# Mixture-of-experts placing on one core: one-hot tables stored with a group's ten picks innermost

## What is computed

```
x = x + segment_sum(norm(x)[src] * edge_weight, dst) @ W.T + b                 # 100000 edges
x = x + ffn on the half of the nodes that a router picks
x = x + relu(segment_sum((norm(x) @ W_rel[type])[src] * gate * w, dst))        # 16 relations
# the last stage: mixture of 8 experts, two per node
gate_logits = norm(x) @ Wg + bg
top_w, top_i = top_k(gate_logits, 2); top_w = softmax(top_w)
out = sum over e of w_dense[:, e] * (gelu(norm(x) @ W1[e] + b1[e]) @ W2[e] + b2[e])
```

## Time and profile before

| What | Value |
|---|---|
| Median of 3 runs | 4001.26 us |
| Lowest and highest of the runs | 3999.29 and 4010.76 us |
| Profiled execution: span from the first to the last recorded instruction | 3402.6 us |
| Profiled execution: its own time around the span | not recorded; the median is 598.7 us above the span |
| Mean granted TensorE clock | 0.902 |
| Busy share: PE, weight loads, DVE, ACT, POOL | 77%, 56%, 51%, 21%, 55% |
| First gather, about | 79 to 1118 us |
| Second gather's loops, about | 1661 to 2670 us |
| Placing | 2678 to 2731 us |
| Experts | 2732 to 3402 us |

### The profile page before, as it was taken

One profiled execution on the slowest core, in us unless ns is written; L12 is line 12 of the kernel. 1 busy time (PEld: TensorE's weight loads), 2 busy tenths in 40 slices (PEclk: granted clock), 3 DMA queues, 4 the chain that ended last, 5 costly groups with the idle time before them and its releaser, 6 DMA issues. The chain is left out here.

```text
span 3402.6 us, 59974 instructions
## 1 busy us (share of the span) xinstructions
PE 2615.4 (77%) x14271; PEld 1921.6 (56%) x14272; DVE 1733.1 (51%) x5663; ACT 723.6 (21%) x1907; POOL 1869.7 (55%) x1915
## 2 busy tenths in 40 slices
PE   7688888887777799999655555564555389999997
PEld 6577777776665344444344444443444267767774
DVE  6455545454554655555355454544544544545553
ACT  4121111111110233333211010000000233333332
POOL 1777777777774000000377777777777245555554
PEclk9899999998999899999888888777777689999998
DMA  7333333333332444444545454555544623222232
GB/s 224 110 113 113 113 111 111 113 113 113 110 113 67 173 197 192 188 191 194 194 141 155 151 154 142 152 154 151 146 146 146 241 59 48 45 45 48 45 48 33
DMA packets 175589, 434.08 MB, mean 128 GB/s; under 512 B 41712, under 2 KB 103792, under 8 KB 169232
## 3 DMA queue, kind: packets, MB, share of 16 engines
q0 software_dynamic: 97072, 236.21, 26.9%
q1 hardware_dynamic: 57424, 183.78, 14.1%
q10 hardware_dynamic: 21008, 13.24, 1.3%
HBM read 275.05 MB, written 158.04 MB: 127 GB/s over the span
## 5 line engine op out<-in xcount | busy, mean ns | idle before, releaser
L776 POOL DMA_INDIRECT g_msg<-table,idx x1564 | 1517.3, 970 | 518.8 <-issue 476.5
L848 PE MATMUL psum<-g_msg,g_hot 128*128 x3328 | 967.4, 456 | 593.0 <-SPq L719 358.1
L848 PEld LDWEIGHTS psum<-g_msg,g_hot 128*128 128x128 f32 x3328 | 756.5, 233 | 789.5 <-issue 654.5
L796 DVE TENSOR_SCALAR g_hot<-iota,g_cols 128x128 f32<-128x128 f32 x1664 | 450.1, 364 | 31.9 <-DVE g_cols L793 30.5
L1908 POOL DMA_INDIRECT out<-ex_y,ex_to x112 | 206.0, 1839 | 253.9 <-DMA out<-ex_y,ex_to 165.3
L768 POOL MEMSET g_origin<- 128x256 f32 x1 | 0.3, 313 | 590.8 <-POOLq L1359 590.8
L1594 PE MATMUL psum<-wrel_halves,t_xhi 128*128 128x512 f16 x784 | 298.2, 380 | 1.7 <-DVE t_row L1475 1.7
L1595 PE MATMUL psum<-wrel_halves,t_xhi 128*128 128x512 f16 x784 | 298.1, 380 | 0.0
L1596 PE MATMUL psum<-wrel_halves,t_xlo 128*128 128x512 f16 x784 | 298.1, 380 | 0.0
L1475 DVE TENSOR_SCALAR t_row<-psum,t_gate 128x256 f32<-128x256 f32 x392 | 171.2, 479 | 233.7 <-PE psum L1596 231.7
L2074 PE MATMUL psum<-w,ex_ghi 128*128 x784 | 260.6, 382 | 6.7 <-DVE ex_y L1983 6.4
(11 more groups left out here) (353 smaller groups left out, 3231.7 us busy)
## 6 DMA issues: line engine op xcount, KB each, us to landing
table<-t_row SPq DMA_DIRECT2D x48, 2048.0 KB, 6.3
g_msg<-table,idx POOLq DMA_INDIRECT x1564
piece_stage<-in_w SPq DMA_DIRECT2D x32, 512.0 KB, 5.7
w_halves<-piece_halves SPq DMA_DIRECT2D x32, 512.0 KB, 3.4
w<-w_halves SPq DMA_DIRECT2D x8, 2048.0 KB, 22.6
rows<-sc_row ACTq DMA_DIRECT2D x50, 128.0 KB, 2.2
out<-acc ACTq DMA_DIRECT2D x49, 128.0 KB
table<-t_row SPq DMA_DIRECT2D x24, 256.0 KB, 2.5
```

The lines of the kernel that those rows point to most:

```text
L776: pool.indirect_dma_start(out=msg[:, at:at + D], out_offset=None, in_=table, in_offset=bass.IndirectOffsetOnAxis(ap=t[f"idx{g}"][:, n:n + ...
L796: last = nc.vector.tensor_scalar(hot[b][:, k * P:(k + 1) * P], t["iota32"][:, :], c3[:, k, where:where + 1], c3[:, k, weight:weight + 1], ...
L848: pe.matmul(ps, hot[b % PAIR][:, k * P:(k + 1) * P], msg[:, bass.ds(slot_at[k], D)], start=False, stop=False, skip_group_check=True).then_ ...
```

## The change

The innermost axis of `hot_tile`, `hot_row` and `parts` becomes the pick within the group (`LANES` is 10), for all groups; `by_lane` gives that view. ACT writes once a table `lanes` of 128 x 10 float16, in which each number stands ten times, and DVE compares it with the picks, which are now read with step one along the innermost axis and with step zero along the middle one. ACT's five instructions per group read and write pairs of float16 with a step of 20 bytes between the pairs. Both operands of PE's matmuls have a step of 20 bytes between elements. Besides, single register loads become `value_load`, and three wait values per batch on PE are masked with 1023.

```diff
@@ slot_number
-        _, (n,) = nc.values_load_multi_w_load_instructions(slot_at(m, 0, 1), engines=[eng.engine], min_val=0, max_val=WINDOWS,
-                                                           skip_runtime_bounds_check_because=sure)
-        return n
+        return eng.value_load(slot_at(m, 0, 1), min_val=0, max_val=WINDOWS)
@@ gather, tensor
-                    pe.wait_ge(tiles_in, code[MSG_TILES])
+                    pe.wait_ge(tiles_in, code[MSG_TILES] & 1023)
...
-                            pe.wait_ge(bank_free, code[BATCH + k // BANKS] + 1)
+                            pe.wait_ge(bank_free, (code[BATCH + k // BANKS] & 1023) + 1)
@@ gather, close_from
-                    _, (n,) = nc.values_load_multi_w_load_instructions(
-                        t["closed"][0:1, bass.ds(m, 1)], engines=[act.engine], min_val=0, max_val=WINDOWS - 1 - k,
-                        skip_runtime_bounds_check_because=sure)
+                    n = act.value_load(t["closed"][0:1, bass.ds(m, 1)], min_val=0, max_val=WINDOWS - 1 - k)
@@ class Place
+    LANES = GROUP * TOP
...
+        self.lanes = late.sb("pl_lanes", [P, P * self.LANES], F16)
...
+    def by_lane(self, x, n):
+
+        return x[:, :].rearrange("p (q s) -> p q s", s=self.LANES)[:, :, 0:n]
@@ Place.vector
+        dve.wait_ge(self.lanes_made, 1)
...
-                nc.vector.tensor_tensor(hot_[:, 0:n * width].rearrange("p (s q) -> p s q", q=width), t["iota16"][:, 0:width].unsqueeze(1).to_broadcast([P, n, width]),
-                                        pick[:, first:first + n].unsqueeze(2).to_broadcast([P, n, width]), ALU.is_equal).then_inc(done, 1)
+                nc.vector.tensor_tensor(self.by_lane(hot_, n), self.by_lane(self.lanes, n)[:, 0:width, :],
+                                        pick[:, first:first + n].unsqueeze(1).to_broadcast([P, width, n]), ALU.is_equal).then_inc(done, 1)
@@ Place.scalar
+        nc.scalar.activation(self.by_lane(self.lanes, self.LANES), t["iota16"][:, :].unsqueeze(2).to_broadcast([P, P, self.LANES]), ACT.Copy).then_inc(self.lanes_made, 1)
         act.wait_ge(self.exp_ready, 1)
...
-                cut = slice(k * TOP * PLACE_COLS, (k + 1) * TOP * PLACE_COLS)
-                last = nc.scalar.activation(self.parts[b][:, cut], self.hot_tile[b][:, cut], ACT.Copy, scale=self.const["number"][:, n % self.CYCLE:n % self.CYCLE + 1])
+                to, of = (self.by_lane(x[b], self.LANES)[:, :, k * TOP:(k + 1) * TOP] for x in (self.parts, self.hot_tile))
+                last = nc.scalar.activation(to, of, ACT.Copy, scale=self.const["number"][:, n % self.CYCLE:n % self.CYCLE + 1])
@@ Place.tensor
-                last = pe.matmul(self.psN[:, to * PLACE_COLS:(to + 1) * PLACE_COLS], self.hot_row[b][:, s * P:(s + 1) * P],
-                                 self.parts[b][:, s * PLACE_COLS:(s + 1) * PLACE_COLS],
+                last = pe.matmul(self.psN[:, to * PLACE_COLS:(to + 1) * PLACE_COLS], self.by_lane(self.hot_row[b], self.LANES)[:, :, s],
+                                 self.by_lane(self.parts[b], self.LANES)[:, :, s],
```

More of the change, by code:

```diff
@@ L1681, in __init__ @@
         (self.link, self.consts_in, self.hot_ready, self.exp_ready, self.exped, self.summed, self.facts_ready, self.facts_stored,
-         self.tile_done, self.row_done, self.parts_done, self.mm_done) = core.sems(*(f"pl_{k}" for k in (
-            "link", "consts_in", "hot_ready", "exp_ready", "exped", "summed", "facts_ready", "facts_stored", "tile_done", "row_done", "parts_done", "mm_done")))
+         self.tile_done, self.row_done, self.parts_done, self.mm_done, self.lanes_made) = core.sems(*(f"pl_{k}" for k in (
+            "link", "consts_in", "hot_ready", "exp_ready", "exped", "summed", "facts_ready", "facts_stored", "tile_done", "row_done", "parts_done", "mm_done", "lanes_made")))
         self.psD, self.psT, self.psN = core.bank[6], core.bank[7], core.bank[0]
+    def by_lane(self, x, n):
+        return x[:, :].rearrange("p (q s) -> p q s", s=self.LANES)[:, :, 0:n]
     def sync(self, sp):
```

## The result

| | before | after |
|---|---|---|
| median, us (4 runs each) | 4006.01 (3999.29 to 4012.14) | 4038.88 (4033.08 to 4049.62) |
| profiled execution: span, us | 3402.6 | 4041.8 |
| granted TensorE clock, mean | 0.902 | 0.816 |

A forecast was written before the change was run, and what follows sets the result against it. The prediction took POOL to pace the gathers and the facts' store behind the weight stream to end the placing. Terms -0.06 (earlier store) and +0.5 (register loads) gave +0.4 us on 4001.26: 4001.7 us, range 3997 to 4016.

The forecast's parts named there:

- the register loads: Checked loads add 0.17 us each, hidden beside POOL in the loops, bare only behind the last fetch: +0.5 us, bounds 0 to 1.5.
- The three masks per batch on PE are one register operation each, beside POOL too: 0: PE's masked wait values in the gathers: hidden beside POOL, 0 us, and 0.1 at the last batch.
- what DVE, PE and ACT do beside them costs nothing: Gathers run at POOL's pace, so the other engines' work beside the fetches is free until the last fetch is out.
- the three signs by which I wanted to see myself wrong: PE or DVE last at the barrier, L1801 over 0.62 us, or the release more than 2 us earlier.
- POOL's waits as before: Sign of being right: POOL in the gathers still waits for nothing but its own issuing between 1563 of 1564 fetches.
- register loads come bare in the loops: Rival: 108 loads at 0.17 us on PE cost 18 us, 4020 us, if POOL waits for ring buffers; chance 0.02.
- The rival on ACT's stepped pairs: Placing, L1801: 1.27 us per copy gives +33 us, 4034 us; chance 0.10 for over 12 us, 0.08 for 3 to 12.
- the compares: DVE's two compares per group in the placing run at twice the rate: 0.82 and 0.74 us, from 1482 and 1317 ns.
- the ramp: One ACT instruction of 1280 elements, 1.3 us, written some 17 us before DVE asks for it: costs nothing.
- DVE's 12.4 us: DVE's own work in the placing falls by 10 x 1.24 us, hidden by the weight stream and the store behind it.
- PE may take up to the pace, 2.6 to 2.7 us, at no cost: Placing: PE's ten loads and matmuls, 1.09 us per group, stay under 2 us with stepped operands, hidden behind ACT and the store.
- the 1.24 forecast: The facts' store is issued 1.24 us earlier, behind the first group's faster compares; term -0.06 us at the end.

The follow-up runs named there:

- 4000 group: Kernels timed together in which every kernel took 3950 to 4110 us, the kernel before 3997 to 4051 us.
- after_again: The change itself, timed again in a group with the kernel before at 3996.85 us: 4045.07 us, ratio 1.0118.
- after_lean: The change with slot number and closed window loaded unchecked and bounded by masks, against the kernel before at 3996.85 us: 4033.80 us, ratio 1.0099.
- 3400 group: Kernels timed together in which every kernel, the kernel before included, took about 3400 us.
- after_third: The change itself once more, in a group with the kernel before at 3402.45 us: 3403.55 us, ratio 1.0001.
- regs_only: The kernel before with the change's three register edits and none of its placing, kernel before at 3399.90 us: 3400.51 us, ratio 1.0007.
- regs_again: The kernel before with only the change's register edits, timed again, kernel before at 3996.85 us: 4047.93 us, ratio 1.0132.

## Why the prediction was wrong

**Where the time goes.** In one 4000 group the change is 48 us above before and its register work alone 51, the same within the spread. With 0.058 us per operation, PE's three masks per batch are 3 x 208 x 0.058 = 36 us, an estimate as rough as that price; the 11 us between `after_again` and `after_lean` go with the assertions and their subtractions on PE, DVE and ACT, which no run here splits by engine. Together 47.

**The step that failed** is in the register loads: "The three masks per batch on PE are one register operation each, beside POOL too: 0", and with it the sentence that "what DVE, PE and ACT do beside them costs nothing". It rests on the earlier trace rows, a row of an execution of 3402.6 us, which I set against a median 598.7 us above it and "leave as it is". Those 598.7 us were the warning: a gather that takes 1.5 times as long isn't paced by a POOL whose own instructions take the same time. In the runs that were timed POOL waits some 600 us and more for PE (655 in the trace of after), and each operation on PE's queue is on the path in part. Taken for its own kind of run the forecast holds: in a 3400 group I gave +0.4 us, and the change measured 1.1 with a ratio of 1.0001, which is no difference that could be told from none. None of the three signs by which I wanted to see myself wrong came up, since all three looked at the placing; the one that did show it, "POOL's waits as before", stood among the signs of being right.

**The rival** "register loads come bare in the loops" had the mechanism, its place and its condition (POOL waits for ring buffers), at 4020 us. Its chance of 0.02 was the mistake of judgement, since the one row against it came from the other kind of run. It was undersized too: it counted PE's 108 loads and not the 624 masks, which by the estimate above carry more than the loads do. That the rival on ACT's stepped pairs named +33 us, the measured number, is luck: its copies would have had to take 1.27 us, and they took 0.49.

**Point by point, the placing.** Right: the compares (0.82 and 0.74), ACT between 0.47 and 0.60 (0.49), the ramp hidden (1.27 us, at about the 1.3 forecast), ACT last at the barrier because of the facts' store, nothing of DVE's 12.4 us at the end. Wrong: ACT still waits for `hot_tile` (14.3 us, before 15.4), and PE's ten matmuls take 2.22 us, not under 2. "PE may take up to the pace, 2.6 to 2.7 us, at no cost" was wrong as a mechanism too, since PE's time is part of the round of 5.29 us. With the old 1.09 us in it the round would be 4.16, or 2.08 per group (an estimate), which is the pace I had forecast; it stayed at 2.65, and only the store hid that. The store itself gains nothing: it is issued 21.2 us behind the weights' start instead of 21.6 (2704.60, `after_third`, less 2683.37; before 2701.99 less 2680.43), and then takes 30.8 us, not 29.9. One pair of traces says little here, so all twelve of the 3400 kind: 21.6 to 22.5 us in the seven with the old layout, 20.9 to 21.2 in the five with the new. That is about 1 us sooner, near the 1.24 forecast. But the store takes 29.0 to 30.0 us in the old and 30.8 to 31.5 in the new, and the release comes 51.8 to 52.8 us behind the weights' start in the old (mean 52.1) and 52.4 to 52.7 in the new (mean 52.6). The ranges overlap, but nothing of the earlier issue is left at the release. Why the store takes longer stays open, and half a microsecond is too little for the medians to show. Timeline and DMA issue, `after_third`:

```profile
2704.60 0.41 ACTq L1810 DMA_DIRECT2D rows<-facts  x1
```
```profile
rows<-facts ACTq DMA_DIRECT2D x1, 100.0 KB, 30.8
```

PE's stepped columns did pay, 1.09 to 2.22 us per group, and ACT's pairs nearly nothing, 0.469 to 0.493. The rule of the Trainium skill that I weighed, in "SBUF — State Buffer", section "Door 1: The DMA port swizzle", has full rate for two hits per 16-byte line and a price for each crossing to a new one. The trace agrees with it, and the cover kept it from the end.

## What to carry to other kernels

A profile whose span is far from the median tells of another kind of run: no wait or missing wait in it may price anything at zero, and the first question is which engine would be the bound if the difference were real. An engine that is "never waited for" can still be only a microsecond or two per turn away; then every register operation in a loop counts, and it is the count per turn on the nearest engine that matters, not the loads that look expensive. Where a sequencer is the bound, raising a value already in its table and loading registers in one instruction are cheap ways to win.

## What was not expected of the hardware

- One kernel, two speeds: `regs_only` at 3400.51 and, as `regs_again`, at 4047.93 us, every kernel of a group alike. PE's gaps are the largest visible part, 316 us of "issue" before L1064's matmuls, but register operations on DVE, ACT and SP stretch to 0.7 and 1.4 us as well, and POOL's don't. The cause isn't in the profile.
- PE's queue takes 0.1 us per register operation though one lasts 36 ns. Two that follow each other in `regs_only`, 704.9 to 705.3 us:

```profile
L844 PEldq ALU_OP  x2: 32/34/36, 705.0 to 705.1; - x2
```

- A load of 8 registers takes 1.94 us, one of 11 takes 1.33 and one of 19 takes 1.83: its time isn't a price per register.
- Both PE operands with 20 bytes between elements: ten f16 matmuls in 2.22 us against 1.09 when contiguous, at a granted clock of 0.50 in both and a matmul's mean of 384 ns against 294. The weight loads' mean is 143 ns against 139; no run steps one operand alone, so which of the two pays isn't shown.
